# Three pairs of score banks, xn on GpSimd, and masks between the halves of a selection

## The reference

```
x = x + attention(layernorm(x))                      # 16 heads, causal
xn = rmsnorm(layernorm(x)) * gamma
sim[p] = q[p] . keys[p]                              # p = 0, 1; 8 heads, 32 keys each
sx, ix = top_k(sim[0], 16);  sy, iy = top_k(sim[1], 16)
scores, pk = top_k(sx[:, None] + sy[None, :], 16)    # the 16 best pairs of a head
h = gelu(xn . table_down[indices]) * softmax(scores)
x = x + sum(h * table_up[indices])
```

## Time and profile before

| | us |
|---|---|
| median of 3 runs (1209.47, 1212.75, 1215.9) | 1212.75 |
| the profiled execution | 1214.8 |
| its span, first to last instruction | 1213.0 |
| DVE busy | 992.3 (82%) |
| PE busy | 881.6 (73%) |
| ACT busy | 713.9 (59%) |
| POOL busy | 607.3 (50%) |

### The profile page before, as it was taken

One profiled execution on the slowest core, in us unless ns is written; L12 is line 12 of the kernel. 1 busy time (PEld: TensorE's weight loads), 2 busy tenths in 40 slices (PEclk: granted clock), 3 DMA queues, 4 the chain that ended last, 5 costly groups with the idle time before them and its releaser, 6 DMA issues.

```text
span 1213.0 us, 20292 instructions
## 1 busy us (share of the span) xinstructions
PE 881.6 (73%) x5298; PEld 451.2 (37%) x5298; DVE 992.3 (82%) x4082; ACT 713.9 (59%) x993; POOL 607.3 (50%) x339
## 2 busy tenths in 40 slices
PE   4779687785867678686867868586786858677454
PEld 3234243342524334252433425253442525243232
DVE  2146897888979888888988889898888889887887
ACT  1436656575656657565665756566575656557353
POOL 1011845638184564818366481836548183653731
PEclk9976868696878969687787969878796977879665
DMA  5010102001010100101010010102011010100000
GB/s 137 1 30 1 30 2 35 0 12 22 5 29 0 33 0 16 18 5 29 0 33 0 18 16 5 29 0 33 0 20 14 5 29 0 29 1 5 1 5 5
DMA packets 36938, 19.72 MB, mean 16 GB/s; under 512 B 3632, under 2 KB 36528, under 8 KB 36720
## 3 DMA queue, kind: packets, MB, share of 16 engines
q1 hardware_dynamic: 36912, 19.42, 8.7%
HBM read 13.64 MB, written 5.24 MB: 16 GB/s over the span
## 4 chain that ended last, share of the span: by engine, by line
PE 38%; DVE 38%; issue 12%; ACT 9%; DMA 1%; DVEq 1%; SPq 0%; ACTq 0%
DVE prob L858 10%; PE score L1126 8%; ACT prob L581 5%; PE att L1053 5%; PE misc L1145 4%; PE att L1055 4%; DVE cand L801 3%; DVE late_scores L714 3%; DVE gated_t L879 3%; DVE left L784 3%; PE misc L1095 2%; PE misc L1075 2%; PE att L1023 2%; PE score L1102 2%; DVE y_t L729 2%
## 5 line engine op out<-in xcount | busy, mean ns | idle before, releaser
L398 POOL TENSOR_TENSOR acc<-acc,prob 128x1024 f32<-128x1024 f32 x186 | 438.5, 2357 | 14.1 <-DVE prob L858 1.4
L858 DVE SCALAR_TENSOR_TENSOR prob<-score,cut,prob 128x1024 f32<-128x1024 f32 x256 | 323.8, 1280 | 112.8 <-ACT prob L581 111.9
L581 ACT ACTIVATE prob<-score,neg_lse,unit 128x1024 f32<-128x1024 f32 x256 | 304.7, 1203 | 161.9 <-PE score L1126 121.5
L1126 PE MATMUL score<-sel,pieces_t 128*128 128x512 f16 x512 | 185.6, 451 | 110.3 <-DVE prob L858 109.9
L398 POOL TENSOR_TENSOR acc<-prob 128x1024 f32<-128x1024 f32 x31 | 73.1, 2357 | 224.3 <-DVE prob L858 224.3
L1023 PE MATMUL att<-k_stack,q_stack 48*128 48x256 bf16 (+1 forms) x512 | 108.2, 329 | 31.1 <-ACT halves L494 31.1
L511 ACT ACTIVATE probs<-att 128x512 f32<-128x512 f32 x192 | 109.6, 596 | 35.6 <-PE att L1055 34.2
L1126 PEld LDWEIGHTS score<-sel,pieces_t 128*128 128x128 f16 x512 | 39.9, 107 | 219.7 <-DVE prob L858 195.9
L1102 PE MATMUL score<-xn_t,wdt 128*128 128x256 f32 x256 | 80.3, 469 | 39.4 <-DVE gated_t L879 39.4
L352 POOL TENSOR_TENSOR rstd<-ln_tmp,half_neg 128x2 f32<-128x2 f32 x16 | 11.6, 725 | 179.8 <-DVE ln_tmp L694 179.8
L494 ACT ACTIVATE late_scores<-att 128x512 bf16<-128x512 f32 x128 | 76.4, 597 | 34.5 <-PE att L1026 34.5
(11 more groups left out here) (109 smaller groups left out, 1428.3 us busy)
## 6 DMA issues: line engine op xcount, KB each, us to landing
q_stack<-q_scratch SPq DMA_DIRECT2D x96, 64.0 KB
q_scratch<-qk_piece SPq DMA_DIRECT2D x16, 192.0 KB, 2.4
xin<-x SPq DMA_DIRECT2D x16, 128.0 KB, 5.4
xres<-x SPq DMA_DIRECT2D x16, 128.0 KB, 2.2
out<-fin SPq DMA_DIRECT2D x16, 128.0 KB, 1.8
k_stack<-qk_piece SPq DMA_DIRECT2D x96, 4.0 KB
prob<-consts SPq DMA_DIRECT2D x1, 1216.0 KB, 6.5
prob<-wq SPq DMA_DIRECT2D x1, 512.0 KB, 5.1
```

The source lines that it names most:

```text
L398: eng.tensor_tensor(acc[:, j, :], so_far, prob[:, j * FH + h, :], ALU.add).then_inc(acc_added, 1)
L581: eng.activation(prob[:, g, :], score[g % 2][:, :], ACT.Exp, bias=neg_lse[:, j, h:h + 1], scale=unit[:, :]).then_inc(prob_made, 1)
L858: eng.scalar_tensor_tensor(prob[:, g, :], score[g % 2][:, :], cut[:, j, h:h + 1], prob[:, g, :], ALU.is_ge, ALU.mult).then_inc(prob_masked, 1)
L1126: ins = eng.matmul(score[g % 2][:, cols], pieces_t[:, j, h, :], sel[:, cols], start=True, stop=True)
```

## The change

- **PSUM.** `score` has three bank pairs (BUFS = 3), and head g uses `score[g % 3]`: its matmuls wait for the mask of head g-3. The two `att` banks are the halves of `score[2]`, so both passes of the attention scores, the hidden layer and the heads 2, 5, 8, 11 and 14 share it in turn. scores_for_max waits for mask 14 of the batch before, the hidden layer's first half for the last copy of that pass, scores_for_probs for the second Gelu, head 2 for the last attention Exp. `project_y` writes `misc[1]`.
- **Hidden layer.** Two units by tile (8 matmuls of 128 columns each, on `score[2]`) in place of two of 4 chunks of 256 columns on `score[0]` and `score[1]`. The first Gelu stands before `pieces_back` on ACT, and the Gelu table is loaded before the wait.
- **xn on POOL.** `make_xn` on POOL makes the scale as before and then, after a wait for it, the two TENSOR_SCALARs that DVE ran.
- **DVE's order.** select_keys(0), select_pairs(0), gate(0), sum_best(0), all folds, gate(1), ln1, log_sum_exp(0), select_keys(1), finish, masks 0 and 1, select_pairs(1), qk_remainder, sum_best(1), masks 2 and 3, log_sum_exp(1), masks 4 and 5, make_y, masks 6 and 7, make_x2, masks 8 to 15.
- **PE and ACT** follow: both expert_outputs stand between score units, all 12 attention Exps stand before the Exp of head 2, and the Exp of heads 0 and 1 before those of scores 4 and 6.

The diff, cut to its core and moved left by eight columns:

```diff
@@ -157,8 +158,8 @@
-score = [ctx.enter_context(nc.psum_tensor(f"score{n}", [P, EXPERTS], FP32)) for n in range(2)]
-att = [ctx.enter_context(nc.psum_tensor(f"att{n}", [P, BANK], FP32)) for n in range(2)]
+score = [ctx.enter_context(nc.psum_tensor(f"score{n}", [P, EXPERTS], FP32)) for n in range(BUFS)]
+att = [score[2][:, n * BANK:(n + 1) * BANK] for n in range(2)]
 misc = [ctx.enter_context(nc.psum_tensor(f"misc{n}", [P, BANK], FP32)) for n in range(2)]
@@ -368,13 +369,21 @@
-    def scale(b):
+    def make_xn(b):
...
             eng.wait_ge(xn_made, at(xn_made, b, 0))
+        if later(b):
+            eng.wait_ge(xn_tp, at(xn_tp, b, 0))
         eng.tensor_tensor(scale2[:, :], bounded[:, :], half_neg[:, :], ALU.pow).then_inc(scale2_made, 1)
+        value = held(eng, every(scale2_made, b))
+        eng.wait_ge(setup_pool, 1)
+        eng.wait_ge(scale2_made, value)
+        for j in range(TILES):
+            eng.tensor_scalar(xn[:, j, :], x2[:, j, :], mv2[:, j, 0:1], scale2[:, j:j + 1],
+                              ALU.subtract, ALU.mult).then_inc(xn_made, 1)
@@ -545,14 +554,16 @@
-    def activate(b, n):
-        eng.wait_ge(hidden, at(hidden, b, n + 1))
-        if later(b):
-            eng.wait_ge(gated, at(gated, b, 0))
-        eng.activation(act_t[:, 4 * n:4 * n + 4, :].rearrange("p c t -> p (c t)"),
-                       score[n][:, :], ACT.Gelu).then_inc(act_made, 1)
-        if n == 1:
+    def activate(b, j):
+        if j == 0:
+            eng.preload_act_table_set("gelu_and_others")
+        eng.wait_ge(hidden, at(hidden, b, j + 1))
+        if later(b):
+            eng.wait_ge(gated, at(gated, b - 1, j + 1))
+        eng.activation(act_t[:, :, j * P:(j + 1) * P], score[2][:, :].rearrange("p (c t) -> p c t", t=P),
+                       ACT.Gelu).then_inc(act_made, 1)
+        if j == 1:
             eng.preload_act_table_set("natural_log_exp_and_others")
@@ -611,52 +622,50 @@
             log_sum(i, 0)
+            activate(i, 0)
             pieces_back(i, 0)
...
         if f:
-            activate(i, 0)
             activate(i, 1)
         if a:
-            for u in range(4):
-                att_exp(i + 1, u)
+            att_exp(i + 1, 0)
+            att_exp(i + 1, 1)
         if p:
...
         if a:
+            att_exp(i + 1, 2)
+            att_exp(i + 1, 3)
+        if f:
+            pair_probs(i, 0, 0)
+        if a:
             att_exp(i + 1, 4)
...
         if f:
-            pair_probs(i, 0, 0)
+            pair_probs(i, 0, 1)
         if a:
...
             att_exp(i + 1, 7)
-        if f:
-            pair_probs(i, 0, 1)
-        if a:
-            att_exp(i + 1, 8)
-            att_exp(i + 1, 9)
         if p:
...
             v_back(i + 2)
+        if a:
+            for u in range(8, MAX_STEPS):
+                att_exp(i + 1, u)
         if f:
             best_exp(i, 1)
-        if a:
-            att_exp(i + 1, 10)
-            att_exp(i + 1, 11)
-        if f:
             pair_probs(i, 0, 2)
-            pair_probs(i, 0, 3)
         if p:
...
         if f:
+            pair_probs(i, 0, 3)
+            log_sum(i, 1)
             for h in range(4, FH):
                 pair_probs(i, 0, h)
-            log_sum(i, 1)
             copy_x2(i)
-            for h in range(3):
+            for h in range(4):
                 pair_probs(i, 1, h)
-            pair_probs(i, 1, 3)
         if a:
@@ -756,15 +770,6 @@
         eng.tensor_tensor(bounded[:, :], mv2[:, :, 1], bounded[:, :], ALU.max).then_inc(ln2_step, 1)
-    def make_xn(b):
-        eng.wait_ge(scale2_made, every(scale2_made, b))
-        eng.wait_ge(ln2_step, every(ln2_step, b))
-        if later(b):
-            eng.wait_ge(xn_tp, at(xn_tp, b, 0))
-        for j in range(TILES):
-            eng.tensor_scalar(xn[:, j, :], x2[:, j, :], mv2[:, j, 0:1], scale2[:, j:j + 1],
-                              ALU.subtract, ALU.mult).then_inc(xn_made, 1)
@@ -919,20 +924,17 @@
         make_x2(0)
-        make_xn(0)
...
             select_pairs(i, 0)
-        if a:
-            fold_max(i + 1, 0, 1)
-        if f:
-            sum_best(i, 0)
         if d:
             gate(i - 1, 0)
-        if a:
-            fold_max(i + 1, 1, 6)
+        if f:
+            sum_best(i, 0)
+        if a:
+            fold_max(i + 1, 0, 6)
         if d:
@@ -940,33 +942,34 @@
             select_keys(i, 1)
-            select_pairs(i, 1)
         if d:
...
             mask(i, 0, 1)
+            select_pairs(i, 1)
         if p:
...
             sum_best(i, 1)
-            for h in range(2, FH):
-                mask(i, 0, h)
+            mask(i, 0, 2)
+            mask(i, 0, 3)
             log_sum_exp(i, 1)
+            mask(i, 0, 4)
+            mask(i, 0, 5)
         if a:
...
         if f:
+            mask(i, 0, 6)
+            mask(i, 0, 7)
+        if a:
+            make_x2(i + 1)
+        if f:
             mask(i, 1, 0)
-        if a:
-            make_x2(i + 1)
-        if f:
-            mask(i, 1, 1)
-        if a:
-            make_xn(i + 1)
-        if f:
             if not a:
+                mask(i, 1, 1)
                 add_late_head(1)
-            for h in range(2, FH):
+            for h in range(1 if a else 2, FH):
                 mask(i, 1, h)
@@ -1009,13 +1012,12 @@
         if u == 0:
-            if later(b):
-                eng.wait_ge(att_probs, at(att_probs, b, 0))
+            if isinstance(b, int) and b == 1:
+                eng.wait_ge(att_probs, every(att_probs, 0))
+            elif later(b):
+                eng.wait_ge(prob_masked, at(prob_masked, b - 2, TILES * FH - 1))
             eng.wait_ge(stack_in, every(stack_in, b))
-        elif u == 1:
-            if later(b):
-                eng.wait_ge(x2_made, at(x2_made, b, 0))
-        else:
+        elif u > 1:
             eng.wait_ge(max_kept, at(max_kept, b, u - 1))
@@ -1042,7 +1044,10 @@
         if u < 2:
-            eng.wait_ge(max_kept, every(max_kept, b))
+            if later(b):
+                eng.wait_ge(act_made, every(act_made, b - 1))
+            else:
+                eng.wait_ge(max_kept, every(max_kept, b))
         else:
@@ -1095,12 +1101,16 @@
-    def hidden_chunks(b, n):
-        if later(b):
-            eng.wait_ge(gated, at(gated, b - 1, n + 1))
-        for c in range(4 * n, 4 * n + 4):
-            ins = eng.matmul(score[n][:, (c % 4) * T:(c % 4 + 1) * T], wdt[:, c * P:(c + 1) * P],
-                             xn_t[:, :], start=True, stop=True)
+    def hidden_units(b, j, a):
+        if j == 1:
+            eng.wait_ge(act_made, at(act_made, b, 1))
+        elif a:
+            eng.wait_ge(max_kept, every(max_kept, b + 1))
+        else:
+            eng.wait_ge(prob_masked, at(prob_masked, b - 1, TILES * FH - 1))
+        for c in range(CH):
+            ins = eng.matmul(score[2][:, c * P:(c + 1) * P], wdt[:, c * P:(c + 1) * P],
+                             xn_t[:, j * P:(j + 1) * P], start=True, stop=True)
         ins.then_inc(hidden, 1)
@@ -1112,24 +1122,29 @@
-    def pair_scores(b, j, h):
+    def pair_scores(b, j, h, a):
...
         if g < 2:
-            eng.wait_ge(act_made, at(act_made, b, g + 1))
+            if later(b):
+                eng.wait_ge(gated, at(gated, b - 1, g + 1))
+        elif g == 2 and a:
+            eng.wait_ge(att_probs, every(att_probs, b + 1))
+        elif g == 2:
+            eng.wait_ge(act_made, every(act_made, b))
         else:
-            eng.wait_ge(prob_masked, at(prob_masked, b, g - 1))
+            eng.wait_ge(prob_masked, at(prob_masked, b, g - 2))
         for half in range(2):
             cols = slice(half * BANK, (half + 1) * BANK)
-            ins = eng.matmul(score[g % 2][:, cols], pieces_t[:, j, h, :], sel[:, cols],
+            ins = eng.matmul(score[g % BUFS][:, cols], pieces_t[:, j, h, :], sel[:, cols],
                              start=True, stop=True)
...
-        eng.wait_ge(prob_masked, at(prob_masked, b, TILES * FH - 1 + j))
+        eng.wait_ge(prob_masked, every(prob_masked, b))
         if j == 1 and isinstance(b, int) and b == BATCHES - 1:
@@ -1166,87 +1181,88 @@
...
         if a:
-            for u in range(MAX_STEPS):
+            for u in range(6):
                 scores_for_max(i + 1, u)
...
             acc_transposes(i - 1, 0)
-        if f:
+        if a:
+            for u in range(6, MAX_STEPS):
+                scores_for_max(i + 1, u)
+        if f:
+            hidden_units(i, 0, a)
             piece_transposes(i, 0)
...
             acc_transposes(i - 1, 1)
-        if f:
-            hidden_chunks(i, 0)
         if a:
...
         if f:
-            hidden_chunks(i, 1)
+            hidden_units(i, 1, a)
+        if a:
+            scores_for_probs(i + 1, 0)
+            scores_for_probs(i + 1, 1)
         if d:
             expert_output(i - 1, 0, i if f else i - 1)
-        if a:
-            for u in range(4):
-                scores_for_probs(i + 1, u)
         if p:
...
         if a:
+            scores_for_probs(i + 1, 2)
```

(36 more changed lines are left out.)

55 lines of the change are left out of this document (29 added, 26 removed).

## The result

The changed kernel takes **1173.19 us** in the median of four runs (1168.87 to 1177.57), the kernel before beside it 1211.94 (1209.47 to 1215.9). The ratio is 0.9677, with a 95% interval of 0.9632 to 0.9723. The forecast was 1187. The time falls between it and the rival "released one add earlier" (1154). The profiled execution has a span of 1170.5 us at a mean granted clock of 0.781.

A forecast was written before the change was run, and what follows sets the result against it. POOL's adds, then a chain through selection, maximum and attention scores, were taken to set the period: 31.1 + 37.8 = 68.9 against 70.78 us. Over 14 periods that gives -26, the last batch -1: 1187 us, range 1150 to 1223.

The forecast's parts named there:

- released one add earlier: Rival: DVE's cand sums are freed while POOL's last add still runs; period 66.5 us, time 1154 us, chance 0.25.
- pair 2 started behind C+29: Sign of being wrong: PE starts head 2's pair over 29 us after DVE starts size for tile 0; forecast 27.9.
- Q to C: From POOL starting qk_low_piece (Q) to DVE next starting size for tile 0 (C): 37.8 us forecast, 39.37 before.
- C to Q: From DVE starting size for tile 0 (C) to POOL starting qk_low_piece (Q): 31.1 us forecast, 31.4 before.
- What bounds it: POOL's adds hold DVE's cand sums and so set the period; DVE savings between Q+13.5 and C alone give nothing.
- T1: Experiments' theory: period is C to Q plus Q to C, which ends with POOL's instruction releasing the last cand sum.
- term (a): On POOL after scale: xn's wait and two instructions at 0.31 us each add 0.8 us (0.5 to 1.6).
- (b): POOL's idle time before scale falls from 2.67 to 1.6 us: -1.1 us (-1.6 to +0.5).
- (c): POOL's idle 1.03 us before the sim_low pieces disappears: -1.0 us.
- The masks: DVE's masks end at Q+26.0, 3.7 us earlier than before, with 3.8 us added for late masks 13 to 15.
- Masks 8 to 15 and the third pair: cost and gain nothing: On DVE: masks end 3.7 us earlier, but DVE waits that time at cand for POOL's last three adds.
- The slower rival: Rival: PE's and ACT's chain grows, C to Q 33.7 us, period 71.5, time 1223 us, chance 0.15.

The follow-up runs named there:

- experiment 5: Changed kernel, with POOL's last three adds of tile 1 waiting until DVE has made the next batch's cand sums: 1112.74 us.
- experiment 6: Changed kernel, with POOL's last three adds of tile 1 cut to 8 of their 1024 columns: 1081.95 us.
- experiment 7: Changed kernel, with the last three adds behind the next cand sums and select_pairs(1) back before finish and masks 0 and 1: 1122.91 us.
- experiment 8: The same kernel as experiment 7, run once more for a profile: 1123.1 us.
- experiment 9: Kernel before, with xn on POOL and POOL's last three adds behind the next batch's cand sums: 1174.05 us.
- experiment 10: Kernel before, with only POOL's last three adds moved behind the next batch's cand sums: 1216.34 us.
- experiment 11: Changed kernel, with the last three adds behind the next cand sums and head g waiting for mask g-2: 1162.61 us.
- experiment 12: Kernel of experiment 5, with xn on POOL as two two-input instructions over 256 elements, the subtraction ahead of the pow: 1128.8 us.
- Experiment 3: Changed kernel, with three bank pairs kept but head g's matmuls waiting for mask g-2 instead of g-3: 1231.19 us.
- Experiment 1: Kernel before, with xn made on POOL and nothing else changed: 1183.24 us.
- experiment 4: Changed kernel, with select_pairs(1) back in front of finish and masks 0 and 1: 1166.17 us.
- experiment 2: Changed kernel, with xn back on DVE behind mask 8 and only the scale made on POOL: 1181.0 us.

## Why the prediction was right or wrong

By the prediction's own signs its mechanism is half right: `cand` was released before the last add, and pair 2 started behind C+29. What happened from Q to C is the rival "released one add earlier", to which 0.25 had been given. That the forecast came within 14 us of the time is in part luck: per period Q to C was 1.5 us shorter than forecast and C to Q 0.9 longer, and the 8.3 us of the first period were not foreseen at all. The stated range took in all three rivals.

**What bounds it** held where POOL's adds stand before `cand`. There `cand` is held by POOL, and DVE's savings count only in steps of one of POOL's instructions: Q to C is 37.6 for xn alone and 40.4 for two deep, 2.4 of it one add and the rest the later end of sim_low. Elsewhere sim_low's end (experiments 5 to 9) or the masks' (10 to 12) sets C, and T1's sums mostly missed. The prediction's rule that a DVE instruction with all operands in SBUF waits for POOL is too wide: the MAX8 of the lists, all in SBUF, take 0.17 to 0.2 us under POOL's pieces as elsewhere. Nor does one instruction slip in behind every POOL instruction: one does between two adds, which lie 0.08 us apart, and none behind a sim_low piece that the next instruction follows without a gap (the second `cand` above is held at once).

**Q to C, term (a)**: wrong in size. I priced a tensor_scalar on POOL by half of a two-input product, 0.31, and took 0.15 to 0.7 as its bounds. It takes 0.80, outside of them; with the gap the step costs 1.76, where I had 0.8. By the rule of the Trainium skill ("GPSIMD Engine Reference", section 4.1 Engine selection) that I weighed, the two-input figure gave 0.67, an estimate and the nearer one; its statement that one input runs at about line rate does not fit this instruction, which has one tensor input and two per-partition scalars: 0.80 against DVE's free 0.33. **Terms (b) and (c)** held: 1.46 idle before scale (1.6 forecast), none before sim_low. **The masks** were 1.0 us too late in the forecast, Q+25.0 for Q+26.0. Masks 8 to 11 run back to back; the last four wait 2.8 in all, not 3.8. **The decision between forecast and rival** was therefore lost on two small terms of the same direction: xn moved sim_low's end from Q+30.5 to Q+31.3, the masks moved `cand` to Q+30.7, and `cand` came 0.6 us ahead of it instead of 1.2 behind. Either term alone would have left it behind, by 0.4 or 0.2. The threshold of the rival (masks before Q+24.8) had been worked out with the cheap xn; with sim_low ending at Q+31.3 it is 31.3 - 5.66 = Q+25.7, and the masks were ahead of it. Its price of 35.4 became 36.3 by the same xn.

**"Masks 8 to 15 and the third pair: cost and gain nothing"**: wrong. Experiment 3 shows 58 us. The step that failed is its conclusion: I looked only for what earlier masks give at `cand`, where POOL's last add seemed to wait for nobody. But masks 3 to 7 stand ahead of make_x2, and with two deep pairs POOL stands 3.32 instead of 1.46 before scale, and sim_low and the adds go with it. Experiment 1, also two deep but in the order of the kernel before, has a period of 68.3 with only 13.6 us to scale: so what the third pair pays for is, at least in part, the new order. That this comes from where masks 3 to 7 stand in it was argued, not separated.

**C to Q**: 32.0 for 31.1. The half clock, which I had put at most on expert 0 (31.6), lies over hidden_units(1) (2.67) and expert 0 (3.07):

```profile
439.90:447.90 8.00, 6.71 (x34) 5.35 (x34) 7.81 (x74) 3.77 (x5) 1.93 (x3) 0.57 0.01 1
```

```profile
439.73 2.67 PE L1112 MATMUL score<-xn_t,wdt 128*128 128x128 f32 x16
...
443.69 0.58 PE L1058 MATMUL score<-q_stack,k_stack 49*128 49x512 bf16 x1 [1.29 <-ACT act_t L564]
...
445.26 3.07 PE L1160 MATMUL misc<-wu,gated_t 128*128 128x128 f32 x16
...
458.97 0.60 PE L1141 MATMUL score<-sel,pieces_t 128*128 128x512 f16 x2 [0.69 <-ACT probs L520]
```

max_t is at C+10.15, as forecast, the first score unit (443.69) at C+13.8 (12.35), and pair 2 (the last row) at C+29.1 (27.9). Expert 1 takes 1.95 as I had it, but finish waits for it until C+22.1, not C+20. At full clock C to Q is 29.6 (the iteration at 907.41 under experiment 4), 1.5 us shorter than forecast: the 31.1 lay between the two levels of the clock, and the clock decided. The slower rival had this mechanism; its point of decision, 33.0, was not reached. That the placing fills a wait and shortens nothing (C to Q) held for this kernel's time only because of the half clock: at full clock it is worth 0.9 us here (experiment 4) and in experiments 7 and 8.

**The sum** by the measured terms is 32.0 + 36.3 = 68.3, -2.5 for -1.9 per period, which over 14 of them makes -35. **"The first period has no earlier batch"**: wrong in its conclusion, by 8.3 us. C to Q in it is 35.3 before and 29.4 after, and the difference is in the granted clock. Before (first fence) and after (second), 12 us from C+15 on:

```profile
103.20:115.20 12.00, 9.94 (x24) 3.18 (x25) 10.18 (x75) 9.59 (x15) 0.04 (x1) 0.59 0.00 1
```

```profile
104.70:116.70 12.00, 9.90 (x40) 3.97 (x40) 10.12 (x78) 11.15 (x19) 2.35 (x1) 1.00 0.01 1
```

In the same busy time PE does 40 matmuls where it did 24, since the clock is 1.00 for 0.59. No part of the change gives this alone. Experiment 1 (xn moved, old order) keeps 73.1 for this period and experiment 2 (all but xn) 72.6, and both have the half clock in it. Experiments 3 and 4, with two deep pairs and with the old placing, have C to Q at 29.4 and 29.1 and the full clock, so this part needs neither the third pair's slack nor the placing: it is xn's move together with the new order. **The last batch** was forecast -1 and gave -1.1.

**Left open**: why the granted clock falls where it falls. In the changed kernel it fell in hidden_units(1), behind 4 us (435.90 to 439.90) at full clock in which PE was busy for 0.55; more than such rows isn't shown. It changed with edits elsewhere (experiments 5, 6, 7 and 12 missed their expected times by 25 to 33 us, two faster and two slower), and the gains of different edits don't add up.

## What to carry to other kernels

Where a DVE instruction takes several times its shortest duration, find the POOL instruction that ends with it, and ask which one would release it if DVE came a little earlier: gains come in steps of one such instruction. Put long POOL work that nobody waits for beside DVE work that it doesn't hold (here MAX8 lists and the masks with their PSUM operand); one wait that does this gave 60 us, more than the whole change, but only in an order where the first fold stood mostly clear of it. Before a shorter stretch is credited to an edit, compare TensorE's clock in it in both traces. Price an instruction that changes engine by a row of its own kind on that engine, or take a range that goes past the neighbours; and work out a rival's threshold again for both ends of that range.
